# The first kernels in halves, and a convolution's Toeplitz rows for both heads in one transfer

## The reference

```
kernel[h] = 2 Re sum_n Cs[h,n] exp(dtA[h,n] * l)          # 64 heads, 1,024 taps each
y  = causal convolution of (x * mask) with kernel, + D x, * mask
x1 = x + attention(y)                                     # 32 heads of 32, 8 key/value heads, Wq Wk Wv Wo
x2 = per-sequence channel mix of x1 (64 x 64 matrices chosen by a condition)
out = x1-mixed through W_base + top-2-of-8 low-rank experts
```

## Time and profile before

| | |
|---|---|
| median of 3 runs | 904.31 us (903.91 to 904.40) |
| the profiled execution's own time | 903.88 us, span 902.0 us |
| TensorE busy | 877.8 us, 97% |
| VectorE, ScalarE, GpSimd busy | 436.1, 202.6, 400.0 us |
| TensorE's granted clock | full (2.4 GHz) in all 40 slices |
| bytes moved | 105.35 MB, mean 117 GB/s |

### The profile page before, as it was taken

How to read it: one execution, slowest core, us unless ns; L and a number is a source line. 1 busy time by engine, 2 the same in 40 slices (tenths; PEclk the granted TensorE clock), 3 DMA queues, 4 the chain that set the end, 5 groups by cost and what they waited for, 6 DMA issues and landing times.

```text
span 902.0 us, 24817 instructions
## 1 busy us (share of the span) xinstructions
PE 877.8 (97%) x10982; PEld 764.5 (85%) x10982; DVE 436.1 (48%) x917; ACT 202.6 (22%) x366; POOL 400.0 (44%) x309
## 2 busy tenths in 40 slices
PE   2999999999999999999999999999999999999998
PEld 2999999988888888887777777777789999999997
DVE  6565551111222222269887777788534433334444
ACT  4455542100000000033222222233331101111010
POOL 3444564203555556569977888777511000000000
PEclk9999999999999999999999999999999999999999
DMA  3788778112224222265544454543452121221201
GB/s 82 195 218 223 190 196 188 60 47 70 71 70 105 70 71 71 55 191 163 146 139 129 159 170 144 160 150 114 162 165 79 48 94 72 72 77 66 94 25 71
DMA packets 83402, 105.35 MB, mean 117 GB/s; under 512 B 41696, under 2 KB 54880, under 8 KB 83296
## 3 DMA queue, kind: packets, MB, share of 16 engines
q1 hardware_dynamic: 80304, 102.73, 38.5%
q10 hardware_dynamic: 2480, 0.51, 0.3%
q0 software_dynamic: 512, 0.53, 0.2%
HBM read 74.08 MB, written 29.65 MB: 115 GB/s over the span
## 4 chain that ended last, share of the span: by engine, by line
PE 89%; POOL 4%; DVE 3%; DMA 2%; issue 1%; SPq 0%; ACT 0%; DVEq 0%; POOLq 0%
PE ps L1329 21%; PE ps L1139 20%; PE ps L867 19%; PE ps L569 10%; PE ps L831 5%; PE ps L580 5%; PE ps L1095 3%; PE ps L1075 2%; PE ps L1302 2%; POOL rf L978 1%; PE ps L1352 1%; POOL rot L974 1%; DMA raw_cols<-in_dram 1%; PE ps L1353 1%; POOL sc L1166 1%
## 5 line engine op out<-in xcount | busy, mean ns | idle before, releaser
L1329 PE MATMUL ps<-wb,xf 128*128 128x420 f32 (+1 forms) x1152 | 195.8, 330 | 0.0
L1329 PEld LDWEIGHTS ps<-wb,xf 128*128 128x128 f32 x1152 | 188.3, 188 | 2.8 <-issue 0.2
L867 PE MATMUL ps<-y_hi,w_hi 128*128 128x512 f32 x320 | 125.1, 391 | 0.0
L867 PE MATMUL ps<-y_hi,w_lo 128*128 128x512 f32 x320 | 124.6, 389 | 0.0
L867 PE MATMUL ps<-y_lo,w_hi 128*128 128x512 f32 x320 | 124.6, 389 | 0.0
L1139 PE MATMUL ps<-y_hi 128*128 128x512 f32 x256 | 103.0, 402 | 0.9 <-POOL y_lo L1002 0.9
L1139 PE MATMUL ps<-y_hi,y_lo 128*128 128x512 f32 x256 | 100.2, 391 | 0.0
L1139 PE MATMUL ps<-y_lo,y_hi 128*128 128x512 f32 x256 | 100.2, 391 | 0.0
L569 PE MATMUL ps<-xc,toep 64*128 64x192 f32 (+4 forms) x1088 | 96.7, 330 | 1.5 <-DVE ym L654 0.6
L569 PEld LDWEIGHTS ps<-xc,toep 64*128 64x128 f32 x1088 | 91.0, 187 | 4.5 <-issue 2.2
L974 POOL TENSOR_TENSOR rot<-rot,cst 128x512 f32<-128x512 f32 x40 | 53.7, 1343 | 72.8 <-DVE rot L945 72.8
(11 more groups left out here) (153 smaller groups left out, 1260.6 us busy)
## 6 DMA issues: line engine op xcount, KB each, us to landing
toep<-kpad SPq DMA_DIRECT2D x62, 272.0 KB, 4.9
xc<-in_dram SPq DMA_DIRECT2D x32, 256.0 KB, 4.2
q_rows<-rf SPq DMA_DIRECT2D x32, 256.0 KB, 2.8
q<-q_rows SPq DMA_DIRECT2D x16, 512.0 KB, 4.0
xr<-in_dram SPq DMA_DIRECT2D x16, 512.0 KB, 4.4
x_scratch<-xr SPq DMA_DIRECT2D x16, 512.0 KB, 2.6
x<-x_scratch SPq DMA_DIRECT2D x16, 512.0 KB, 3.5
out_dram<-x SPq DMA_DIRECT2D x15, 512.0 KB, 2.6
```

The lines of the kernel that those rows point to most:

```text
L867: mm = pe.matmul(kq_bank(n), w[a][:, j, :], yt[b][:, j, g * 512:(g + 1) * 512], start=(j == 0 and a + b == 0), stop=(j == NJ - 1 and a == 1))
L1329: mm = pe.matmul(joint_bank(i, piece)[:, 0:hi - lo], xf[i % 2][:, a, t, :], wb[t][:, w4_place(t, c), lo:hi], start=(t == 0 and a + c == 0) ...
```

## The change

- Group 0 is made in two halves of four heads, 128 columns each, as "steps" 0 and 1; groups 1 to 7 are steps 2 to 8. `phases` is split into `phase_turns` and `phase_fractions`. VectorE does the first half's tables, then the turns of the second half, then takes out the first half's taps. The product for the right table stays on GpSimd, in halves.
- Head numbering changes: turn n takes heads n//2*4 + n%2 and two above it, so the first half feeds turns 0 and 1.
- Each half's taps are stored in four transfers of one head each, in the order 0, 2, 1, 3; a turn waits for its two stores.
- A turn's rows (all turns but 0) are still two transfers, but each brings half of the columns, 544, for both heads: 2 heads x 64 rows.
- Group 1's matmuls move from behind turn 0 into turn 1, ahead of its last matmuls; its angles come after the second half's taps.
- In `first_tables` two products wait for four links of GpSimd's chain in place of its end.
- `wo_lo(7)` moves on GpSimd ahead of the last `subtract_max` and rotation of stage 2. In attention `turn_probs` comes second, `maximum` fourth.

```diff
-        st_zero, st_k = signal("st_zero"), signals("st_k", 2 * GP)
+        st_zero, st_first, st_k = signal("st_zero"), signals("st_first", GP), signals("st_k", 2 * XH)
...
+        def step_of(g):
+
+            return g + 1
+
+        def step_heads(step):
+            return slice(step * GP, (step + 1) * GP) if step < 2 else slice((step - 1) * HGRP, step * HGRP)
+
+        def step_cols(step):
+            return slice(step * P, (step + 1) * P) if step < 2 else slice(0, GC)
+
+        def sines(act, step):
+            act.wait_ge(v_round, 3 * (step + 1))
+            part = step_cols(step)
             for i in range(3):
-                act.activation(rn[:, i, :], rn[:, i, :], ACT.Sin, scale=-SIN_SCALE,
+                act.activation(rn[:, i, part], rn[:, i, part], ACT.Sin, scale=-SIN_SCALE,
...
-            gp.wait_ge(a_sin, 3)
-            gp.tensor_tensor(rtab, rn[:, 2, :], mg[:, 1, :], ALU.mult).then_inc(g_rtab, 1)
+            for step in range(2):
+                gp.wait_ge(a_sin, 3 * (step + 1))
+                part = step_cols(step)
+                gp.tensor_tensor(rtab[:, part], rn[:, 2, part], mg[:, 1, part], ALU.mult).then_inc(g_rtab, 1)
...
+        def phase_turns(v, step):
+
+            part = step_cols(step)
             for i, r in enumerate(("v32", "vr")):
-                v.tensor_tensor(ph[:, i, :].rearrange("p (h s) -> p h s", s=HB), along(M(r)[:, hs], HB),
-                                          across(C("step"), HGRP), ALU.mult).then_inc(v_ph, 1)
-            v.wait_ge(v_ph, 5 * g + 2)
-            for i, part in enumerate((0, 0, 1)):
-                v.tensor_scalar(rn[:, i, :], ph[:, part, :], C("off")[:, i:i + 1], ROUND, ALU.add, ALU.add).then_inc(v_ph, 1)
-            v.wait_ge(v_ph, 5 * g + 5)
-            for i, part in enumerate((0, 0, 1)):
-                v.scalar_tensor_tensor(rn[:, i, :], rn[:, i, :], ROUND, ph[:, part, :],
-                                                    ALU.subtract, ALU.subtract).then_inc(v_round, 1)
+                v.tensor_tensor(ph[:, i, part].rearrange("p (h s) -> p h s", s=HB), along(M(r)[:, step_heads(step)], HB),
+                                across(C("step"), (part.stop - part.start) // HB), ALU.mult).then_inc(v_ph, 1)
+            v.wait_ge(v_ph, 5 * step + 2)
+            for i, half in enumerate((0, 0, 1)):
+                v.tensor_scalar(rn[:, i, part], ph[:, half, part], C("off")[:, i:i + 1], ROUND, ALU.add, ALU.add).then_inc(v_ph, 1)
+
+        def phase_fractions(v, step):
+
+            part = step_cols(step)
+            v.wait_ge(v_ph, 5 * step + 5)
+            for i, half in enumerate((0, 0, 1)):
+                v.scalar_tensor_tensor(rn[:, i, part], rn[:, i, part], ROUND, ph[:, half, part],
+                                       ALU.subtract, ALU.subtract).then_inc(v_round, 1)
+
+        def phases(v, step):
+            phase_turns(v, step)
+            phase_fractions(v, step)
...
-            v.wait_ge(g_fac, 1)
+            v.wait_ge(g_set, 4)
             v.scalar_tensor_tensor(M("u"), M("u"), 2.0, M("den"), ALU.mult, ALU.mult)
             chain(v, v.scalar_tensor_tensor(M("w"), M("w"), 2.0, M("den"), ALU.mult, ALU.mult))
+            v.wait_ge(g_fac, 1)
...
+            part, hs = step_cols(step), step_heads(step)
             for i, c in enumerate(("cr", "ci")):
-                v.wait_ge(a_sin, 3 * g + i + 1)
-                w = rn[:, i, :].rearrange("p (h s) -> p h s", s=HB)
+                v.wait_ge(a_sin, 3 * step + i + 1)
+                w = rn[:, i, part].rearrange("p (h s) -> p h s", s=HB)
                 chain(v, v.tensor_tensor(w, w, along(M(c)[:, hs], HB), ALU.mult))
-            chain(v, v.tensor_tensor(rn[:, 0, :], rn[:, 0, :], rn[:, 1, :], ALU.subtract))
-            v.wait_ge(a_mag, 2 * (g + 1))
-            if g > 0:
-                v.wait_ge(pe_k, g)
-            if g == 0:
-                v.tensor_tensor(ltab, rn[:, 0, :], mg[:, 0, :], ALU.mult).then_inc(v_tab, 2)
-            else:
-                v.wait_ge(a_sin, 3 * g + 3)
-                v.tensor_tensor(ltab, rn[:, 0, :], mg[:, 0, :], ALU.mult).then_inc(v_tab, 1)
+            chain(v, v.tensor_tensor(rn[:, 0, part], rn[:, 0, part], rn[:, 1, part], ALU.subtract))
+            v.wait_ge(a_mag, 2 if step < 2 else 2 * step)
+            if step >= 2:
+                v.wait_ge(pe_k, step)
+            v.tensor_tensor(ltab[:, part], rn[:, 0, part], mg[:, 0, part], ALU.mult).then_inc(v_tab, 1)
+            if step >= 2:
+                v.wait_ge(a_sin, 3 * step + 3)
                 v.tensor_tensor(rtab, rn[:, 2, :], mg[:, 1, :], ALU.mult).then_inc(v_tab, 1)
+
+        def first_kernels_pe(pe, half):
+            pe.wait_ge(v_tab, half + 1)
+            pe.wait_ge(g_rtab, half + 1)
+            cols = step_cols(half)
+            pe.matmul(ps[:, 6, cols], ltab[:, cols], rtab[:, cols], start=True, stop=True).then_inc(pe_k, 1)
+
+        def first_kernels_out(v, half):
+            v.wait_ge(pe_k, half + 1)
+            k = ksb[:, 0, half:half + 1, :]
+            v.tensor_copy(k, ps[:, 6, step_cols(half)].unsqueeze(1)).then_inc(v_ke, 1)
+            v.wait_ge(v_ke, half + 1)
+            k0 = k.rearrange("p u (i b) -> p u i b", b=HB)[:, :, :, 0]
+            v.tensor_tensor(k0, k0, along(d_at[:, 0, half:half + 1], GP), ALU.add).then_inc(v_k, 1)
+
+        def store_first_kernels(eng, half):
+            eng.wait_ge(v_k, half + 1)
+            heads = kpad.ap()[half * GP:(half + 1) * GP, P - 1:P - 1 + L].rearrange("k (a b) -> k a b", b=HB)
+            for pair in range(XH):
+                for k in (pair, XH + pair):
+                    eng.dma_start(heads[k], ksb[k * HB:(k + 1) * HB, 0, half, k * HB:(k + 1) * HB])\
+                       .then_inc(st_first[half * XH + pair], 16)
...
+            return n // XH * 2 * XH + r * XH + n % XH
...
+        ROW_HALVES = [(0, (L + HALF) // 2), ((L + HALF) // 2, L + HALF)]
...
         def load_toeplitz(sp, n):
             if n - TR + 1 > 0:
                 sp.wait_ge(pe_conv, n - TR + 1)
-            for r in range(2):
-                load_rows(sp, n, r, 0, L + HALF, ld_toep[n % TR])
+            for lo, hi in ROW_HALVES:
+                sp.dma_start(toep[:, n % TR, lo:hi],
+                             bass.AP(kpad, head(n, 0) * (KROW + 1) + lo, [[XH * (KROW + 1), 2], [1, HALF], [1, hi - lo]]))\
+                  .then_inc(ld_toep[n % TR], 16)
 
         def conv_loads(sp):
             for t in range(1, XR):
                 load_x_conv(sp, t)
-            store_kernels(sp, 0)
+            store_first_kernels(sp, 0)
             load_first_toeplitz(sp, 0)
             for n in range(1, S // 2):
-                g = n // GP
+                if n == 2:
+                    store_first_kernels(sp, 1)
...
+                if n == 1:
+                    kernels_pe(pe, 1)
...
-            kernels_pe(pe, 0)
+            first_kernels_pe(pe, 0)
             pe.wait_ge(ld_cst, 16)
             keep_busy(pe, 2, 2 * P)
-            keep_busy(pe, 34, HB)
-            pe.wait_ge(st_k[0], 16)
+            keep_busy(pe, 22, HB)
+            first_kernels_pe(pe, 1)
+            keep_busy(pe, 12, HB)
+            kernels_stored(pe, 0)
...
         def conv_masks(v):
             tables(v, 0)
+            phase_turns(v, 1)
             v.wait_ge(ld_d, 16 * GP)
-            kernels_out(v, 0)
-            phases(v, 1)
+            first_kernels_out(v, 0)
+            phase_fractions(v, 1)
             v.wait_ge(ld_len, 16)
             v.tensor_copy(len_f[:], len_i[:]).then_inc(v_len, 1)
             v.wait_ge(v_len, 1)
             v.tensor_tensor(valid[:], across(len_f[:], NJ), along(C("pos"), NB), ALU.is_gt).then_inc(v_valid, 1)
             v.wait_ge(v_valid, 1)
             tables(v, 1)
+            first_kernels_out(v, 1)
+            phases(v, step_of(1))
+            tables(v, step_of(1))
...
         def conv_hi(act):
+            sines(act, 1)
+            load_first_toeplitz(act, 1)
             magnitudes(act, 1)
-            load_first_toeplitz(act, 1)
-            sines(act, 1)
+            sines(act, step_of(1))
...
                 if lead == 6:
+                    wo_lo(gp, 7)
                     subtract_max(gp, 4)
...
-            wo_lo(gp, 7)
...
                     scale(v, w + CR)
-                    maximum(v, w + CR)
+                if w + 1 < NUNIT:
+                    turn_probs(v, w + 1)
                 if w < NUNIT:
                     o_lo(v, w)
-                if w + 1 < NUNIT:
-                    turn_probs(v, w + 1)
+                if w + CR < NUNIT:
+                    maximum(v, w + CR)
```

More of the change, by code:

```diff
@@ L457, in first_tables, with tables @@
             chain(v, v.tensor_tensor(M("ci"), M("th"), M("k"), ALU.subtract))
-        def tables(v, g):
-            hs = slice(g * HGRP, (g + 1) * HGRP)
+        def tables(v, step):
+            part, hs = step_cols(step), step_heads(step)
             for i, c in enumerate(("cr", "ci")):
-                v.wait_ge(a_sin, 3 * g + i + 1)
```

(55 more changed lines are left out.)

20 lines of the change are left out of this document (7 added, 13 removed).

## The result

The changed kernel takes 1,153.6 us (median of 4 runs, 1,153.4 to 1,155.5) where the kernel before takes 904.1: 1.276 times as long, 95% interval 1.274 to 1.277. The profiled execution took 1,153.78 us, with a span of 1,151.9.

A forecast was written before the change was run, and what follows sets the result against it. TensorE, busy 877.8 of 902.0 us, was taken to bound the kernel, transfers close behind. 903.88 us + 360 (rows on two engines, start's gain included) - 0.9 (weight) gave 1,263 us; range over all cases 900 to 1,345.

The forecast's parts named there:

- two engines: Convolution's row loads: source's outer count of 2 confines them to 2 of 16 DMA engines, 360 us later; chance 0.60.
- I take 18.5: Convolution's row loads: rate of one DMA engine in GB/s, the whole program's mean, giving 15.9 us a turn.
- The first kernels in halves: Start of the kernel: group 0 made in two halves brings 1.6 us, bounds 0.8 to 2.0.
- The other moves at the start I cost at nothing: Start: second half's stores in SyncE's queue and group 1's matmuls inside turn 1, at most half a microsecond lost.
- the one with the start lost: Rows spread over all engines, but the start gives nothing: only 0.9 us or less gained, 903.0 to 904; chance 0.07.
- the one with both gains: Rows spread over all engines, gains of start (1.6 us) and weight (0.9) both kept: 901.4 us; chance 0.25.
- Attention: 0, bounds -0.2 to +0.3: Attention step, VectorE's transpose second and maximum fourth: no gain in us, since TensorE was not waiting.
- The weight: 0.9: Output weight's low half made earlier on GpSimd: TensorE's wait goes, 0.9 us gained, bounds 0.4 to 0.94.

The follow-up runs named there:

- the stores first: Changed kernel with one row load per head, second half's kernels ten small matmuls earlier, their stores on SyncE ahead of turn 1's rows: 901.30 us.
- ScalarE's stores: Changed kernel with one row load per head, second half's kernels earlier and stored by ScalarE, group 1's kernels after turn 1: 907.33 us.
- per-head loads: Changed kernel with only its row loads as before, one load per head of 64 rows of 1,088 numbers, two a turn: 903.28 us.
- both small edits with the old start: Kernel before with the weight's low half moved and VectorE's attention order changed, start and row loads as before: 901.41 us.
- attention alone: Kernel before with only VectorE's order in the attention step changed, transpose of the probabilities second, maximum fourth: 902.76 us.

## Why the prediction came out as it did

The forecast was 1,263 us by two engines; measured 1,153.6, inside that case's own bounds of 1,120 to 1,370. The mechanism was right by most of the points by which it was to be known: TensorE waits in all turns, the DMA share is 2 tenths, the clock falls below 1. The first sign, a landing of the row loads over 10 us, can't be read, since the page prints none for them; the one that can be followed took 21 us, and the inputs 10.0. The convolution lasted 397 us, not some 500. The range over all cases, 900 to 1,345, holds both no loss and this one, so that the time lies inside it says little.

The step that was mis-sized is the rate of one engine, "I take 18.5". That is a mean of a program in which 16 engines work together; two alone do 24.0. I had 26 as the ceiling from the earlier trace rows and put the value near the mean all the same. At 12.6 instead of 15.9 us a turn, 31 turns are 104 us shorter. The rest of the 109: start, landing and last turn took 20.84 + 7.1 where I had 31 (3 us), and behind the convolution 3.2 us were gained (736.9 to 733.7 from the start of the projection to the end) where I had 0.9.

The last turn at half clock took 7.1 us; 8.8 was worked out. The clock cost 2.6 us there and hardly more: in every other turn the matmuls, slow or not, end before the next rows land.

"The first kernels in halves": the first convolution came 1.8 us earlier (20.84 against 22.65), where 1.6 was forecast; in the other kernels with this start and the same small matmuls it began at 20.85 to 21.5. "The other moves at the start I cost at nothing" was the wrong step, hidden in the changed kernel and seen once the loads were spread: the stores in SyncE's queue ahead of turn 2's rows cost 0.9 to 2.7 us there. In the kernels with the new start and spread loads the convolution ended at 165.5, 165.8 and 168.7, in those with the old start at 165.1, 165.2, 166.1 and 166.3; with the stores first it was 164.7, with ScalarE's stores 172.8. The start gives nothing that can be seen in the total. So, among my rivals, the one with the start lost was nearer for spread loads than the one with both gains, which I had given more than three times its chance: with per-head loads the total is 903.28, inside its 903.0 to 904. The 901.4 that the other case forecast is reached by both small edits with the old start, with the gain of attention in place of that of the start.

"Attention: 0, bounds -0.2 to +0.3" was wrong by the 1.4 us of the two gaps, which I had seen on the waits but not counted, since no engine was named for them. "The weight: 0.9" holds within a wide interval: 1.2 us by the times, 0.3 to 2.1. The 0.94 us itself was one execution's: the same wait for GpSimd's low half is 0.3 us in the trace of attention alone and 0.2 in that of the kernel before with the rows together, in both of which the weight was not moved.

## What to carry to other kernels

Before a transfer is merged with its neighbour, read the outer count of both sides: here a count of 2, 4 or 8 outside put the work on that many engines instead of 16, and with 2 longer rows did not bring it back. The number of engines at work is the DMA share times 16 in a stretch where only that transfer moves, and it is the first thing to look at when transfers are late. For the time of a transfer on few engines take the rate at few engines (24 to 25 GB/s each here), not the program's mean (18.5). And a start made earlier is only worth what the second and third turn's data allow: follow the queue past the first use.

## What was not expected of the hardware

One DMA engine moved 24 to 25 GB/s with 2 or 4 at work, 18.7 to 20 with 8 and 15.2 with 16, all with rows of 2,176 or 4,352 bytes out of memory; where other transfers ran beside the rows it moved less. SyncE's issue of a load on two engines lasted 5.2 us in the median, up to 9.1, against 0.6, so the inputs and the second half's stores in its queue were late as well. After a wait of 2.7 us TensorE ran at 1.2 GHz for some 3.5 us in the kernel with per-head loads (clock 0.79, 0.50, 0.85 in the stretches of 2 us from 32 to 38).
